# Gathering the two expert outputs of a token with an accumulating DMA, on one core of Trainium2

## The reference

```
x = x + 0.5 * ffn(layernorm(x))
x = x + attn(layernorm(x))
x = x + 0.5 * ffn(layernorm(x))

ffn(x):  shared  = swiglu(x, ws_gate, ws_up, ws_down)          # 256 hidden channels
         scores  = sigmoid(x @ gate_weight.T)                  # 8 experts
         w, idx  = top_k(scores, 2);  w = 2.5 * w / sum(w)
         out     = shared + sum over the 2 choices of w * swiglu(x, expert idx)   # 128 hidden channels
attn(x): k, v, r = projections of x mixed with the token before it
         state_t = k_t * v_t + exp(time_decay) * state_(t-1)
         out     = layernorm(r * (time_first * k * v + state)) @ Wo.T
```

## Time and profile before

| | |
|---|---|
| Time before, median of 3 runs | 1079.43 us (1076.99 to 1084.72) |
| The profiled execution | 1086.27 us, span 1084.5 us |
| PE busy | 890.7 us (82%) |
| VectorE busy | 787.9 us (73%) |
| GpSimd busy | 680.3 us (63%) |
| ScalarE busy | 588.0 us (54%) |
| Moved by DMA | 198.69 MB |

### The profile page before, as it was taken

The page is one execution under the profiler, slowest core; times in us unless marked ns, Lnnn a source line. Parts: engine busy times, 40 slices in busy tenths (PEclk is TensorE's granted clock), DMA queues, the critical chain, the costliest instruction groups (busy, mean ns, idle before and its releaser), DMA issues.

```text
span 1084.5 us, 24997 instructions
## 1 busy us (share of the span) xinstructions
PE 890.7 (82%) x7800; PEld 637.5 (59%) x7800; DVE 787.9 (73%) x2263; ACT 588.0 (54%) x1395; POOL 680.3 (63%) x669
## 2 busy tenths in 40 slices
PE   1678888779888998999979899889789999886540
PEld 0345665756567565566767676557676755665530
DVE  2676654569887897898678789889488978763342
ACT  7757652664555768663644566644355674433220
POOL 1677574755377467757577437785577267783565
PEclk9789998989998999999999999999999999899885
DMA  8977997993599735445999976576999245999994
GB/s 248 246 205 171 192 240 163 216 246 105 135 173 219 162 107 123 112 114 134 219 227 250 180 161 146 140 202 147 239 207 241 60 117 167 193 231 297 214 250 133
DMA packets 338000, 198.69 MB, mean 183 GB/s; under 512 B 251729, under 2 KB 319953, under 8 KB 337873
## 3 DMA queue, kind: packets, MB, share of 16 engines
q1 hardware_dynamic: 260848, 79.50, 37.4%
q0 software_dynamic: 24576, 67.14, 24.9%
q10 hardware_dynamic: 52448, 50.46, 15.7%
HBM read 47.05 MB, written 92.27 MB: 128 GB/s over the span
## 4 chain that ended last, share of the span: by engine, by line
SPq 24%; PE 20%; issue 14%; DMA 11%; POOL 11%; DVE 9%; ACT 7%; ACTq 3%; POOLq 0%; DVEq 0%
SPq L984 16%; SPq L967 6%; PE ps L1240 6%; DMA xt<-rows 3%; POOL xsB L1062 3%; POOL y_got L1079 3%; DMA y_got<-ysB,y_pos 2%; DMA y_got<-ysA,y_pos 2%; POOL xsA L1062 2%; ACTq L1399 2%; PE ps L1274 2%; DMA xq<-xsB 2%; ACT norm L1378 2%; DVE acc L1514 1%; PE ps L1142 1%
## 5 line engine op out<-in xcount | busy, mean ns | idle before, releaser
L1142 PE MATMUL ps<-xq,w_hi 128*128 128x128 f16 x1248 | 225.4, 225 | 56.4 <-DMA xq<-xsB 29.7
L1144 PE MATMUL ps<-xq,w_hi 128*128 128x128 f16 x1248 | 225.3, 225 | 0.0
L1146 PE MATMUL ps<-xq,w_lo 128*128 128x128 f16 x1248 | 225.0, 225 | 0.0
L1514 DVE SCALAR_TENSOR_TENSOR acc<-y_got,share,acc 128x256 f32<-128x256 f32 x256 | 123.5, 484 | 88.7 <-DMA y_got<-ysB,y_pos 42.3
L1062 POOL DMA_INDIRECT xsA<-rows,pos x128 | 135.4, 1058 | 83.0 <-DVE pos L1640 48.1
L1062 POOL DMA_INDIRECT xsB<-rows,pos x128 | 137.3, 1073 | 60.4 <-issue 35.9
L1079 POOL DMA_INDIRECT y_got<-ysB,y_pos x128 | 132.6, 1036 | 67.0 <-issue 39.4
L1079 POOL DMA_INDIRECT y_got<-ysA,y_pos x128 | 134.4, 1050 | 58.3 <-issue 34.5
L1142 PEld LDWEIGHTS ps<-xq,w_hi 128*128 x1248 | 126.3, 101 | 69.7 <-DMA xq<-xsB 32.6
L1348 ACT CAST hid_h<-hid 128x512 f16<-128x512 f32 (+1 forms) x144 | 87.7, 611 | 128.2 <-PE ps L1173 50.5
L1340 ACT ACTIVATE hid<-ps 128x512 f32<-128x512 f32 (+1 forms) x144 | 83.7, 588 | 112.0 <-PE ps L1146 50.0
(11 more groups left out here) (151 smaller groups left out, 2106.4 us busy)
## 6 DMA issues: line engine op xcount, KB each, us to landing
ysA<-y_sb ACTq DMA_DIRECT2D x36, 512.0 KB
ysB<-y_sb ACTq DMA_DIRECT2D x36, 512.0 KB
acc<-in_x_dram SPq DMA_DIRECT2D x16, 512.0 KB, 6.5
out_dram<-acc SPq DMA_DIRECT2D x16, 512.0 KB, 5.2
xsA<-zeros ACTq DMA_DIRECT2D x36, 128.0 KB
xsB<-zeros ACTq DMA_DIRECT2D x36, 128.0 KB
acc<-in_w_chunks_dram SPq DMA_DIRECT2D x10, 256.0 KB, 4.7
xq<-xsA SPq DMA_TRANSPOSE x156
```

The lines of the kernel that those rows point to most:

```text
L1142: nc.tensor.matmul(half, w_hi[2 * k + b][:, cols], hi, start=(j == 0 and k == 0), stop=False, skip_group_check=True)
L1144: nc.tensor.matmul(half, w_hi[2 * k + b][:, cols], lo, start=False, stop=False, skip_group_check=True)
L1146: mm = nc.tensor.matmul(half, w_lo[2 * k + b][:, cols], hi, start=False, stop=(j == many - 1 and k == KC - 1), skip_group_check=True)
L1514: v.scalar_tensor_tensor(out=acc[:, s, h, :], in0=y_got[:, h, k, :], scalar=share[:, s, h, k:k + 1], in1=acc[:, s, h, :], op0=ALU.mult, op ...
```

## The change

The gather is split in two tasks. `second` gathers the row of the second choice into a buffer of a ring of two for each of the four tiles (`N_GOT = 2`; `y_got` keeps its size). A new task `ratio` on ScalarE multiplies it in place by the ratio of the two weights. Then `gather` gathers the first choice's row onto it with an accumulating indirect DMA (`compute_op=ALU.add`), and `combine` adds the result to `acc` with one instruction, multiplied by the first choice's weight. `top2` keeps the two logits in `share` with one more copy (for B it first waits for the combines of A in that sequence); `route_exp` is now an exponential on ScalarE and `weights` six VectorE instructions, both once for a group. The moments of norm 1 of the first five sequences (`HEAD = 5`) are computed by `stats` on VectorE in place of `sums`. The planner's costs and lags of some tasks, its nominal times and all of its tables are new, and with them the order on every engine. The diff, without the tables and with the unchanged waits left out:

```
+N_GOT = 2
+HEAD = 5
+def by_dve(n, s):
+    return n in "2o" or n == "1" and s < HEAD
...
-    PACE = 34.2
+    PACE = 25.8
...
-        if n != "2":
+        if n != "2" and not by_dve(n, s):
+            after = after + [("norm", ("1", s - 1)) if n == "1" and by_dve(n, s - 1) else None]
             add("act", "sums", (n, s), 4.2, at, after + [("rstd", (n, s - 1)) if s else None],
...
-        add("sp", "turn_rows", (f, s), 5.6, at + 10, [("row_lo", (f, s))], lag=1.6)
+        add("sp", "turn_rows", (f, s), 5.9, at + 10, [("row_lo", (f, s))], lag=2.6)
...
-        add("pool", "route_exp", (f, s), 1.95, at + 21, [("top2", (f, s))])
...
+        add("act", "route_exp", (f, g), 2.9, at - 10, [("top2", fs) for fs in rows])
+        add("dve", "weights", (f, g), 1.35, at - 5, [("route_exp", (f, g))])
...
-            add("sp", "fetch", (f, g, q), 1.46 * blocks_of(f, g, q), at - 10 + gap * q,
-                [("tails", (f, g)), ("table_out", (f, g))] + scattered, lag=2.8)
+            add("sp", "fetch", (f, g, q), 1.45 * blocks_of(f, g, q), at - 10 + gap * q,
+                [("tails", (f, g)), ("table_out", (f, g))] + scattered, lag=4.0)
...
-            add("pool", "gather", (f, s, h), 2.53, at + h,
-                [("y_store", (f, g, q)) for q in range(QUADS[f, g])] + [("y_places", (f, g))], lag=3.2)
-            add("dve", "combine", (f, s, h), 0.98, at + 8 + h, [("gather", (f, s, h)), ("weights", (f, s))])
+            add("pool", "second", (f, s, h), 1.33, at + h,
+                [("y_store", (f, g, q)) for q in range(QUADS[f, g])] + [("y_places", (f, g))], lag=4.4)
+            add("act", "ratio", (f, s, h), 0.46, at + 5 + h, [("second", (f, s, h)), ("weights", (f, g))])
+            add("pool", "gather", (f, s, h), 1.33, at + 6 + h, [("ratio", (f, s, h))], lag=4.6)
+            add("dve", "combine", (f, s, h), 0.46, at + 12 + h, [("gather", (f, s, h)), ("weights", (f, g))])
...
-            def gather(f, s, h):
+            def second(f, s, h):
...
-                if n > 0:
-                    pool.wait_ge(combined, val("combine", *got_by[h][n - 1]))
+                if n >= N_GOT:
+                    pool.wait_ge(combined, val("combine", *got_by[h][n - N_GOT]))
...
-                for k in range(TOPK):
-                    g.indirect_dma_start(
-                        out=y_got[:, h, k, :], out_offset=None, in_=ys[f, g_no],
-                        in_offset=bass.IndirectOffsetOnAxis(ap=y_pos[:, s, h, k:k + 1], axis=0))\
-                        .then_inc(y_in[h], 16)
+                g.indirect_dma_start(
+                    out=y_got[:, h, n % N_GOT, :], out_offset=None, in_=ys[f, g_no],
+                    in_offset=bass.IndirectOffsetOnAxis(ap=y_pos[:, s, h, 1:2], axis=0))\
+                    .then_inc(y_in[h][n % N_GOT], 16)
+
+            def gather(f, s, h):
+                n, g_no = got_by[h].index((f, s, h)), group_of(f, s)
+                pool.wait_ge(scaled, val("ratio", f, s, h))
+                g.indirect_dma_start(
+                    out=y_got[:, h, n % N_GOT, :], out_offset=None, in_=ys[f, g_no],
+                    in_offset=bass.IndirectOffsetOnAxis(ap=y_pos[:, s, h, 0:1], axis=0), compute_op=ALU.add)\
+                    .then_inc(y_in[h][n % N_GOT], 16)
...
+            def ratio(f, s, h):
+                n = got_by[h].index((f, s, h))
+                act.wait_ge(y_in[h][n % N_GOT], 16 * (2 * (n // N_GOT) + 1))
+                act.wait_ge(weights_done, 2 * val("weights", f, group_of(f, s)))
+                nc.scalar.activation(y_got[:, h, n % N_GOT, :], y_got[:, h, n % N_GOT, :], ACT.Copy,
+                                     scale=share[:, s, h, 1:2]).then_inc(scaled, 1)
+
+            def route_exp(f, g):
+                seqs = MEMBERS[f, g]
+                act.wait_ge(logits_kept, max(val("top2", f, s) for s in seqs))
+                if val("route_exp", f, g) > 1:
+                    act.wait_ge(weights_done, 2 * (val("route_exp", f, g) - 1))
+                nc.scalar.activation(score[:, 0:len(seqs) * NT, :],
+                                     share[:, seqs[0]:seqs[-1] + 1].rearrange("p s j k -> p (s j) k"),
+                                     ACT.Exp, scale=-1.0).then_inc(exp_done, 1)
...
-                dve.wait_ge(y_in[h], 16 * TOPK * (n + 1))
+                dve.wait_ge(y_in[h][n % N_GOT], 16 * (2 * (n // N_GOT) + 2))
...
-                for k in range(TOPK):
-                    if k == 1:
-                        dve.wait_ge(first_added, val("combine", f, s, h))
-                    v.scalar_tensor_tensor(out=acc[:, s, h, :], in0=y_got[:, h, k, :],
-                                           scalar=share[:, s, h, k:k + 1], in1=acc[:, s, h, :],
-                                           op0=ALU.mult, op1=ALU.add).then_inc((first_added, combined)[k], 1)
+                v.scalar_tensor_tensor(out=acc[:, s, h, :], in0=y_got[:, h, n % N_GOT, :],
+                                       scalar=share[:, s, h, 0:1], in1=acc[:, s, h, :],
+                                       op0=ALU.mult, op1=ALU.add).then_inc(combined, 1)
...
+                if f == "B":
+                    dve.wait_ge(combined, max(val("combine", "A", s, h) for h in range(PARTS)))
+                v.tensor_copy(share[:, s], best[:, :, 0:TOPK]).then_inc(logits_kept, 1)
```

More of the change, by code:

```diff
@@ L535, in rows_of @@
         add("pe", "rank", (f, s), 0.4, at + 23, [("choose", (f, s))])
-        add("dve", "weights", (f, s), 1.0, at + 25, [("route_exp", (f, s))])
         add("dve", "places", (f, s), 0.92, at + 24,
@@ L540, in rows_of @@
         for j in range(NT):
-            add("pool", "scatter", (f, s, j), 2.6, at + 26, [("places", (f, s))], lag=2.5)
+            add("pool", "scatter", (f, s, j), 2.7, at + 26, [("places", (f, s))], lag=3.2)
     def chunk(what, f, a, b, at, after):
@@ L566, in experts @@
             add("act", "evac", key, 1.0, at + gap * q + 8, [("down", key)])
-            add("act", "y_store", (f, g, q), 0.65, at + gap * q + 9, [("evac", key)], lag=3.6)
+            add("act", "y_store", (f, g, q), 0.45, at + gap * q + 9, [("evac", key)], lag=4.2)
     def gathered(f, s, at):
@@ L631, in takes @@
             return (("bank", uses[name]),)
-        if name == "sums":
+        if name == "sums" or name == "norm" and key[0] == "1" and by_dve(*key):
             return (("norm", 1),)
-        if name == "gather":
+        if name == "route_exp":
+            return (("exp", 1),)
+        if name == "second":
             return ((f"got{key[2]}", 1),)
@@ L678, in frees @@
             gone(("hidden_hi", key), "split", 0)
+        elif name == "weights":
+            gone(("route_exp", key), "exp", 0)
         elif name == "combine":
-            gone(("gather", key), f"got{key[2]}", 0)
+            gone(("second", key), f"got{key[2]}", 0)
         elif name == "y_store":
@@ L688, in follows @@
         name, key = k
-        if name == "sums":
+        if name == "sums" or name == "norm" and key[0] == "1" and by_dve(*key):
             return "rows", None, ("A" if key[0] == "1" else "B", key[1])
-        if name == "norm" and key[0] != "2":
-            return "rows", ("A" if key[0] == "1" else "B", key[1])
-        if name in ("row_hi", "row_lo", "turn_rows", "router", "top2", "route_exp", "choose", "rank",
-                    "weights", "places"):
+        if name in ("row_hi", "row_lo", "turn_rows", "router", "top2", "choose", "rank", "places"):
             return "rows", key
+        if name == "route_exp":
+            return "shares", None, key
+        if name == "weights":
+            return "shares", key
         if name == "gate_up":
@@ L733, in program @@
     row_no = {fs: n for n, fs in enumerate(row_sets)}
-    got_by = [[key for name, key in order["pool"] if name == "gather" and key[2] == h] for h in range(PARTS)]
+    got_by = [[key for name, key in order["pool"] if name == "second" and key[2] == h] for h in range(PARTS)]
     with ExitStack() as ctx:
@@ L859, in program @@
         y_stored = [sem(f"y_stored{b}") for b in range(N_Y)]
-        y_in = [sem(f"y_in{h}") for h in range(PARTS)]
+        y_in = [[sem(f"y_in{h}{b}") for b in range(N_GOT)] for h in range(PARTS)]
+        scaled = sem("scaled")
         tails_in, stored = sem("tails_in"), sem("stored")
@@ L1032, in rstd @@
                 k = s + 1
-                pool.wait_ge(var_done[n], 2 * k if n == "2" else k)
+                pool.wait_ge(var_done[n], sum(2 if by_dve(n, t) else 1 for t in range(k)))
                 if s > 0:
@@ L1403, in norm @@
                 act.wait_ge(rstd_done[n], s + 1)
+                if n == "1" and by_dve(n, s) and row_no["A", s] > 0:
+                    act.wait_ge(row_lo_done, row_no["A", s])
                 to = norm2 if n == "2" else norm32
```

345 lines of the change are left out of this document (171 added, 174 removed), and 250 rows, old and new, of the table SHIFT.

## The result

| | us, median (lowest to highest) | ratio to the kernel before |
|---|---|---|
| before, in the same series | 1081.23 (1076.99 to 1084.72), 4 runs | |
| changed kernel | 1099.09 (1092.38 to 1113.79), 4 runs | 1.0146, interval [1.0076, 1.0216] |
| forecast | 1059 (1030 to 1097) | |

The forecast has the wrong sign. The profiled execution of the changed kernel took 1097.3 us, with a span of 1095.3.

The account below looks back on a forecast made before the run. It saw no single owner of the waits, with PE busy 890.7 of 1084.5 us, so gains had to shorten PE's idle time. Terms summed to -20.5 us: 1086.3 to 1066, less 6.8 for the median, 1059 us, range 1030 to 1097.

Parts of the forecast that it names:

- I take the plain price: Accumulating gathers on POOL: each costs a plain gather's 0.95 us, plus 2 us in all for traffic; upper bound twice that.
- rival 2: POOL's gapless gathers from 918 us on: 39 accumulating ones at double price add 37 us, giving 1096 us; chance 0.21.
- The sign named for this: Accumulating gathers in the trace at 1.5 us or more, instead of about 0.96, would show rival 2.
- The other sign of being wrong: On the chain, new waits of POOL for scaled or ScalarE for y_got of more than some 20 us.
- sum at the plain price: Whole kernel: terms of -10, -12, -3.5, +3 and +2 give -20.5 us, so 1059 us, 1.9% faster; chance 0.42.
- Head: 0 to 108 us: first rows ready about 2 us earlier and half the later waits gone, -10 us, bounds 0 and -21.
- Middle: 108 to 918 us: a third of 37 us of waits by way of VectorE goes, -12 us, bounds 0 and -37.
- Tail: From 918 us: two fewer exponentials before the last scatters, -3 us, and one combine instruction fewer at the end, -0.5.
- ScalarE: +3 forecast: Middle, ScalarE's in-order queue: ratio work and waits lengthen PE's wait for y_sb by some 3 us, bounds 0 and 11.
- POOL's relief of 56 us: POOL loses 32 exponentials of 1753 ns, 56 us, which stood in its order before scatters.
- Rival 1: VectorE's relief is off the path; only 2 us of head and 3 us of tail are won: 1074 us; chance 0.23.
- Rival 3: The new order also closes the tail, the last group's rows coming some 25 us earlier: 1034 us; chance 0.14.

Follow-up runs that it names:

- plain-price run: Changed kernel with its second gather plain, overwriting the buffer instead of accumulating, order and waits kept: 1054.15 us, ratio 0.9778 to the kernel before.

## Why the prediction was wrong

The step that failed is **"I take the plain price"** for the accumulating gather. Its reason was that index list and source bytes are the same, and, under its rival 2, that a scatter, another kind of indirect DMA, cost POOL much the same as a gather (1.07 us beside 0.96; over the whole trace of before a gather is 1.04). The accumulation is another thing: 1.60 us on POOL against 1.03 in the same trace, 1.55 times, and on the DMA engines the upper bound of the working itself, 6.2 points of their time (24.9 to 31.1%). The step stood between two bounds, plain and double, and the sum took the end that was the author's hope; nothing in the trace of before spoke for it. The sign named for this, 1.5 us or more, came.

**Rival 2** came with its sign, and nearly with its time (1096; measured 1099). The time is luck: two errors cancel. Its price was too high: 0.96 us extra, measured 0.57. Its place was too narrow: 39 accumulating DMAs in gapless stretches behind 918 us. From the plain-price run to the changed kernel the span grows by 44.3 us: 16.4 of PE's idle time in the middle, 16.7 behind 918 us, 11.2 of PE's own busy time (the cuts at 108 and 918 us fall at different work in two kernels, so such parts are rough). POOL is 62% busy in the middle, so a gapless stretch isn't what makes its time count. A gather that POOL issues later lands later, and VectorE stands before it in order: the waits of `combine` in the table fit that.

The other sign of being wrong, new waits for `scaled` or y_got above some 20 us on the chain, came as well, but it doesn't set the two kernels apart. On the chain that ended last, 41.9 us in 7 pieces are landings for which `ratio` waited; in the plain-price run, which is faster than before, they are 47.2 us in 9.

The **sum at the plain price** is tested by the plain-price run. Forecast 1.9% faster, measured 2.2%. That the total came so near is in part luck, as the parts show. In PE's idle time against before:

- Head: -10 forecast, -3.8 measured. The first rows came at 22.6 us, not near 20. VectorE's moments began only behind its wait for the constants, which the working had not looked at: it compared 4.4 with 2.5 us of work and not the two starts. The run with that wait moved shows it.
- Middle: -12 forecast, -14.1 with the plain price; +2.3 with the accumulation. The plain-price size came, its path only in part. The forecast took it from xt and from waits for VectorE itself: xt fell by 4.5 us (23.5 to 19.0) and the others by some 2 (16.6 to 14.5, added up over all rows of the view). More came from xq (17.1 to 11.5) and y_sb (10.9 to 4.9), which the forecast left as they were or let grow. The second row of xq before, beside the 11.6 of the earlier trace rows:

```profile
PE ps L1142 <- DMA xq<-xsA: 5.5, 4, 2.8
```

- Tail: -3.5 forecast, -1.3 with the plain price; +15.4 with the accumulation.
- PE's own busy time: no term, -14.3 with the plain price. How much of that is TensorE's clock (mean granted 0.946 against 0.938) stays open.
- ScalarE: +3 forecast, bounds 0 and 11. PE's wait for y_sb in the middle fell from 10.9 to 6.2 us, and the runs without ratio and without table loads show no gain: nothing of the 3 us is to be seen, though the runs could not resolve it.

**Sizes.** VectorE 723 forecast, 727.7 measured; combine 0.48 us as forecast; 17 table loads as forecast; ScalarE 652 forecast, 638.2 measured, the ratio at 506 ns against 496. POOL's relief of 56 us was there (weights per group alone: 59.6). With the 12 us that VectorE lost in that run it was worth about 1.1%, more than the 3 us that the tail got for it, but with an interval that reaches to nothing. Rival 1, which left 1074 us, falls with the 1054 us of the plain-price run. Rival 3's new order did not close the tail.

**Where the gain went, in one line:** the rest of the change is worth some 2%, and the accumulating DMA, with its 73 us on POOL, costs 3.7 points. What is open: why a microsecond on POOL costs about half a microsecond in the new order (40 us for 76) and some 0.8 in the old (58 for 71), and how the last 0.3 to 0.7 points divide between the DMA engines' time and the later landing.

## What to carry to other kernels

A new option on a known instruction is a new instruction: without a row of its own it has no price, and where one word of the code decides the sign, the forecast should sit between its bounds, not at the kind one. An engine with gaps is not off the path when other engines wait in order for what it issues: look at who waits for its products, not at its busy share alone. Work taken off VectorE and paid for on POOL was a bad trade here: with the work back on VectorE and plain gathers on POOL the same result takes 1066 us instead of 1099. Forming the weights per group, with the powers off POOL, gained some 1% by itself, with an interval that reaches to nothing.

## What the runs showed of the hardware

An accumulating indirect DMA of 128 rows takes POOL at least 1.53 us in this trace, 0.95 when plain. POOL's queue shows 48 packets for a plain DMA (24,576 / 512) and 144 for an accumulating one ((36,864 - 384 x 48) / 128). The packets of the queue, scatters among them, took 31.1% of 1095.3 us on the 16 engines, 340.6 us, against 273.3 (26.0% of 1051.0) when all are plain: 67 us more for 128, or 0.53 us each on top of a plain one's 0.53 (273.3 / 512, scatters and gathers taken alike), so double. From the last gather's issue to the start of the last combine it was 3.85 us (1086.22 to 1090.07), before 2.84 (1074.87 to 1077.71); 0.58 of the difference is the longer time on POOL:

```profile
1077.71 1.00 DVE L1514 SCALAR_TENSOR_TENSOR acc<-y_got,share,acc 128x256 f32<-128x256 f32 x2 [1.76 <-DMA y_got<-ysB,y_pos]
```

The Trainium skill (Collectives: The Full Stack, The bandwidth ceiling) says that an addition in the DMA engines needs two source reads, and gives 1.93 as the measured ratio of the bandwidths of a collective that copies and one that adds. The double time of a gather here agrees with it in size; that a second read is the cause no run here shows. What the accumulation costs POOL is the 1.60 us of the trace.
